# Window attention: band mask by a TensorE matmul, exponentials 1024 wide, maxima's rows from GpSimd's queue, longer lags

## What is computed

```python
scores = jnp.einsum('bhqd,bhkd->bhqk', q, k) / math.sqrt(dh)
scores = jnp.exp(scores - jnp.max(scores, axis=-1, keepdims=True))
d = j - i
mask = (d <= half - 1) & (d >= -half)
scores = jnp.where(mask, scores, 0.0)
weights = jax.nn.softmax(scores, axis=-1)
out = jnp.einsum('bhqk,bhkd->bhqd', weights, v)
...
return out.transpose(0, 2, 1, 3).reshape(B, S, H * dh) @ Wo
```

## Time and profile before

| what | value |
|---|---|
| median of 3 executions | 2661.12 us (2660.02 to 2675.28) |
| profiled execution, its own time | 2644.6 us |
| its span | 2642.8 us |
| mean granted TensorE clock | 0.842 |
| TensorE matmuls / weight loads busy | 2100.6 / 1602.7 us |
| VectorE busy | 1811.0 us |
| ScalarE busy | 1392.7 us |
| GpSimd busy | 659.4 us |

### The profile page before, as it was taken

The page is one execution under the profiler, slowest core; times in us unless marked ns, Lnnn a source line. Parts: engine busy times, 40 slices in busy tenths (PEclk is TensorE's granted clock), DMA queues, the critical chain, the costliest instruction groups (busy, mean ns, idle before and its releaser), DMA issues. The chain is left out here.

```text
span 2642.8 us, 46194 instructions
## 1 busy us (share of the span) xinstructions
PE 2100.6 (79%) x13533; PEld 1602.7 (61%) x13533; DVE 1811.0 (69%) x4451; ACT 1392.7 (53%) x2671; POOL 659.4 (25%) x920
## 2 busy tenths in 40 slices
PE   4779888788788898887888668356468848999998
PEld 2345556455555555564555657346467748999997
DVE  3667788778787787787968335536558745777775
ACT  3557667757666676676756212124246533444442
POOL 3110111101111111111100035555521135556511
PEclk8878888989888888898978555667679879999999
DMA  4624643565346435543470081699977742333311
GB/s 72 94 47 67 111 56 62 88 94 70 64 73 111 54 59 94 83 63 70 68 111 18 17 259 70 212 380 341 287 253 248 231 151 84 88 98 100 97 53 39
DMA packets 230094, 306.36 MB, mean 116 GB/s; under 512 B 44445, under 2 KB 145866, under 8 KB 229450
## 3 DMA queue, kind: packets, MB, share of 16 engines
q1 hardware_dynamic: 186746, 199.14, 37.5%
q0 software_dynamic: 22784, 67.13, 7.9%
q10 hardware_dynamic: 20304, 36.97, 3.7%
HBM read 129.33 MB, written 92.27 MB: 84 GB/s over the span
## 5 line engine op out<-in xcount | busy, mean ns | idle before, releaser
L724 DVE CUSTOM_DVE_ANT_0 above<-p_half,above 128x512 f32<-128x512 f32 x1024 | 691.3, 684 | 305.6 <-issue 248.1
L615 ACT ACTIVATE above<-p_diff 128x512 f32<-128x512 f32 x1024 | 599.4, 600 | 269.4 <-PE p_diff L529 267.6
L529 PE MATMUL p_diff<-d_stack,q_stack 96*128 96x512 bf16 x1024 | 433.3, 426 | 127.0 <-ACT above L615 96.0
L533 PE MATMUL p_half<-k_stack,q_stack 96*128 96x512 bf16 x1024 | 431.8, 422 | 31.0 <-DVE row_max L724 27.2
L558 PEld LDWEIGHTS p_pv<-v_win,w_win 128*128 128x128 f32 x2048 | 312.0, 225 | 78.0 <-DVE w_win L758 52.6
L558 PE MATMUL p_pv<-v_win,w_win 128*128 128x34 f32 x2048 | 307.6, 302 | 14.5 <-DVE w_win L758 13.0
L529 PEld LDWEIGHTS p_diff<-d_stack,q_stack 96*128 96x128 bf16 x1024 | 127.0, 125 | 285.3 <-ACT above L615 206.4
L1170 POOL DMA_INDIRECT raw<-sorted_y,place x192 | 206.2, 1074 | 238.5 <-DMA sorted_y<-y_tile 182.9
L641 ACT ACTIVATE p_win<-p_win 128x512 f32<-128x512 f32 x256 | 150.3, 589 | 181.5 <-PE p_win L545 179.9
L421 POOL TENSOR_TENSOR att<-total,inv 128x128 f32<-128x128 f32 x128 | 48.9, 404 | 759.2 <-DVE inv L750 759.2
L1492 ACT ACTIVATE pt_hi<-p_one 128x512 fp32r<-128x512 f32 x128 | 69.6, 595 | 259.6 <-PE p_one L1352 243.9
(11 more groups left out here) (217 smaller groups left out, 4857.1 us busy)
## 6 DMA issues: line engine op xcount, KB each, us to landing
x_tile<-sorted_x SPq DMA_DIRECT2D x141, 256.0 KB
sorted_y<-y_tile ACTq DMA_DIRECT2D x141, 256.0 KB
q_stack<-q_parts SPq DMA_DIRECT2D x256, 96.0 KB, 3.1
k_stack<-k_parts SPq DMA_DIRECT2D x256, 96.0 KB, 3.7
x_in<-in_L_attn_x SPq DMA_DIRECT2D x16, 1024.0 KB, 5.5
x_rows<-x POOLq DMA_DIRECT2D x16, 1024.0 KB
sorted_x<-zeros SPq DMA_DIRECT2D x51, 256.0 KB
d_stack<-d_parts SPq DMA_DIRECT2D x256, 48.0 KB, 3.7
```

The source lines that it names most:

```text
L529: nc.tensor.matmul(p_diff[s % 2][:], qs, d_stack[0:SPLIT_ROWS, h, :], start=True, stop=True).then_inc(s_diff, 1)
L533: nc.tensor.matmul(p_half[s % 2][:], qs, k_stack[g][0:SPLIT_ROWS, h, HALO + S // 2:HALO + S], start=True, stop=True).then_inc(s_half, 1)
L615: nc.scalar.activation(above[:, s % 4], p_diff[s % 2][:], ACT.Relu).then_inc(s_above, 1)
L724: nc.vector.tensor_tensor_reduce(out=above[:, s % 4], in0=p_half[s % 2][:], in1=above[:, s % 4], scale=1.0, scalar=-3.0e38, op0=ALU.add, o ...
```

## The change

The band becomes a bf16 tile `outside`, 0 in the band and -30000 outside. TensorE opens each bank of p_win with a matmul of the identity (bf16) and this tile, 512 columns, and the eight window matmuls of the bank add to it. The first exponential then gives 0 outside the band and the second 1, so VectorE only adds -1, in place in SBUF. Both exponentials are one instruction of 1024 columns, the second writes w_win. The second copies of the parts move from VectorE to GpSimd. The three row DMAs move from SyncE's queue to GpSimd's, behind the low part that they store. The lags change: exponentials 10 and 12, weights 14, weighted values 16 and 17, total 20, reciprocal and products 21.

```diff
-WIN_LAG, TOTAL_LAG, PAIR_LAG = 9, 18, 19
-EXP_LAGS = 10, 11, 12, 13
-WEIGHT_LAGS = 13, 14
-PV_LAGS = 15, 16
+WIN_LAG, TOTAL_LAG, PAIR_LAG = 9, 20, 21
+EXP_LAGS = 10, 12
+WEIGHT_LAG = 14
+PV_LAGS = 16, 17
...
-                if not isinstance(b, int) or 1 <= u <= 2 * B:
-
-                    wait_alone(sp, s_mparts, u)
-                    for part in range(3):
-                        row = SPLIT_ROWS + part
-                        sp.dma_start(q_stack[1 - g][row:row + 1, :, :],
-                                     m_parts[:, part, :]).then_inc(s_mrow, 16)
...
+                            pool.wait_ge(s_mparts, u)
+                            wait(pool, s_win, GH * (u - 2))
+                            alone(pool)
+                            for part in range(3):
+                                row = SPLIT_ROWS + part
+                                pool.dma_start(q_stack[1 - g][row:row + 1, :, :],
+                                               m_parts[:, part, :]).then_inc(s_mrow, 16)
...
+                            copy, of = (0, 1) if kind == "q" else (3, 2)
+                            nc.gpsimd.tensor_copy(parts[:, copy, cols], parts[:, of, cols]).then_inc(s_twice, 1)
...
-                wait(pe, s_ww, 2 * k)
+                wait(pe, s_e2, k)
                 for i in range(NBLK):
                     cols = slice(WIN * i, WIN * i + WIN)
+                    if i % 8 == 0:
+                        bank = p_win[:, 64 * i:64 * i + 512].rearrange("p (i j) -> p i j", j=WIN)
+                        nc.tensor.matmul(bank, ident_b[:], outside[:].unsqueeze(1).to_broadcast([P, 8, WIN]),
+                                         start=True, stop=False, skip_group_check=True)
                     ins = nc.tensor.matmul(p_win[:, cols], k_stack[o][0:ROWS, h, WIN * i:WIN * i + P],
-                                           q_stack[o][0:ROWS, h, cols], start=True, stop=True)
+                                           q_stack[o][0:ROWS, h, cols], start=False, stop=i % 8 == 7,
+                                           skip_group_check=True)
...
                 if again:
-                    act.wait_ge(s_e1, 2 * k + bank + 1)
-                    nc.scalar.activation(p_win[:, cols], p_win[:, cols], ACT.Exp).then_inc(s_e2, 1)
+                    act.wait_ge(s_e1, k + 1)
+                    wait(act, s_pv, k - 1)
+                    nc.scalar.activation(w_win[:, h % 2], p_win[:], ACT.Exp).then_inc(s_e2, 1)
...
-                nc.vector.scalar_tensor_tensor(
-                    w_win[:, h % 2, cols].rearrange("p (i j) -> p i j", j=WIN),
-                    p_win[:, cols].rearrange("p (i j) -> p i j", j=WIN), 1.0,
-                    window[:].unsqueeze(1).to_broadcast([P, NBLK // 2, WIN]),
-                    ALU.subtract, ALU.mult).then_inc(s_ww, 1)
+                dve.wait_ge(s_e2, k + 1)
+                nc.vector.tensor_scalar(w_win[:, h % 2], w_win[:, h % 2], -1.0, None, ALU.add).then_inc(s_ww, 1)
```

More of the change, by code:

```diff
@@ L36 @@
 PROJ = "qkd"
[L39 to L42 removed]
+OUTSIDE = -30000.0
+WIN_LAG, TOTAL_LAG, PAIR_LAG = 9, 20, 21
+EXP_LAGS = 10, 12
+WEIGHT_LAG = 14
+PV_LAGS = 16, 17
 STACK_INC = 16 * 6
@@ L113, in window_attention @@
         ones = sb("ones", [P, 1])
-        window = sb("window", [P, WIN])
+        ident_b = sb("ident_b", [P, P], BF16)
+        outside = sb("outside", [P, WIN], BF16)
         neg_half = sb("neg_half", [P, QT])
@@ L347, in _ @@
             const(nc.gpsimd.memset(ident[:], 0.0))
-            const(nc.gpsimd.memset(window[:], 1.0))
+            const(nc.gpsimd.memset(outside[:], 0.0))
             pool.wait_ge(s_const, 2)
@@ L351, in _ @@
                                           base=0, pattern=[[-1, P]], channel_multiplier=1))
-            const(nc.gpsimd.affine_select(out=window[:], in_=window[:], compare_op=ALU.is_ge, fill=0.0,
+            const(nc.gpsimd.affine_select(out=outside[:], in_=outside[:], compare_op=ALU.is_ge, fill=OUTSIDE,
                                           base=0, pattern=[[-1, WIN]], channel_multiplier=1))
             pool.wait_ge(s_const, 4)
-            const(nc.gpsimd.affine_select(out=window[:], in_=window[:], compare_op=ALU.is_ge, fill=0.0,
+            const(nc.gpsimd.affine_select(out=outside[:], in_=outside[:], compare_op=ALU.is_ge, fill=OUTSIDE,
                                           base=WIN - 1, pattern=[[1, WIN]], channel_multiplier=-1))
@@ L500, in unit @@
                 if g == 1 and has(b, -1, 0):
+                    pe.wait_ge(s_const, 17)
                     pe.wait_ge(s_wlo, 4)
@@ L550, in weighted_values @@
                 k = GH * w + h
-                pe.wait_ge(s_ww, 2 * k + part + 1)
+                if part == 0:
+                    pe.wait_ge(s_ww, k + 1)
                 if h == 0:
@@ L628, in unit, with exponential @@
                                                  ACT.Copy).then_inc(s_mid, 1)
[L629 removed]
+                    for n in (0, 1):
                         for w, o, h in late(b, g, s, EXP_LAGS[n]):
[L631 to L635 removed]
+                            exponential(GH * w + h, h, n)
+            def exponential(k, h, again):
                 if again:
[L637 to L638 removed]
+                    act.wait_ge(s_e1, k + 1)
+                    wait(act, s_pv, k - 1)
+                    nc.scalar.activation(w_win[:, h % 2], p_win[:], ACT.Exp).then_inc(s_e2, 1)
                 else:
                     act.wait_ge(s_win, k + 1)
[L641 removed]
+                    nc.scalar.activation(p_win[:], p_win[:], ACT.Exp, scale=DH ** -0.5).then_inc(s_e1, 1)
             batches(act, unit)
@@ L731, in unit @@
                             job(b, g, j, kind, i)
-                    for j, kind, i in jobs(b, g, s, 4):
-                        if kind in PROJ:
-                            dve.wait_ge(s_mid, before(PROJ, b, g, j) + 1)
-                            parts = {"q": q_parts, "k": k_parts, "d": d_parts}[kind]
-                            copy, of = (0, 1) if kind == "q" else (3, 2)
-                            cols = slice(512 * i, 512 * i + 512)
-                            nc.vector.tensor_copy(parts[:, copy, cols], parts[:, of, cols]).then_inc(s_twice, 1)
-                    for n in (0, 1):
-                        for w, o, hh in late(b, g, s, WEIGHT_LAGS[n]):
-                            weights(GH * w + hh, hh, n)
+                    for w, o, hh in late(b, g, s, WEIGHT_LAG):
+                        weights(GH * w + hh, hh)
                     for w, o, hh in late(b, g, s, TOTAL_LAG):
@@ L751, in unit, with weights @@
                                                  total[:, hh // 2 % 2, :, DH]).then_inc(s_inv, 1)
-            def weights(k, h, bank):
-                cols = slice(512 * bank, 512 * bank + 512)
-                dve.wait_ge(s_e2, 2 * k + bank + 1)
-                wait(dve, s_pv, k - 1)
-                nc.vector.scalar_tensor_tensor(
-                    w_win[:, h % 2, cols].rearrange("p (i j) -> p i j", j=WIN),
-                    p_win[:, cols].rearrange("p (i j) -> p i j", j=WIN), 1.0,
-                    window[:].unsqueeze(1).to_broadcast([P, NBLK // 2, WIN]),
-                    ALU.subtract, ALU.mult).then_inc(s_ww, 1)
+            def weights(k, h):
+                dve.wait_ge(s_e2, k + 1)
+                nc.vector.tensor_scalar(w_win[:, h % 2], w_win[:, h % 2], -1.0, None, ALU.add).then_inc(s_ww, 1)
             def totals(b, w, o, h):
```

13 lines of the change are left out of this document (5 added, 8 removed).

## The result

The change makes the kernel slower: 2746.57 us, the median of 4 executions, against 2663.91 us for the kernel before on the same chip, a ratio of 1.0314 (95% interval 1.0264 to 1.0364), or +82.7 us. The forecast was 2643 us in a range of 2560 to 2712. The profiled execution of the changed kernel took 2746.77 us.

A forecast was written before the change was run, and what follows sets the result against it. No engine was taken as full: heads were TensorE's burst plus VectorE's tail, with VectorE bounding heads with copies. Terms -61.5 - 50 + 102 + 13 - 21 = -17.5 us took the median 2661.1 to 2643 us, range 2560 to 2712.

The forecast's parts named there:

- Rows and copies: Row DMAs and second copies moved to GpSimd: VectorE's rows wait mostly goes, -61.5 us; copies leave VectorE, -50 us.
- Weights: One 1024-wide VectorE weight per head from SBUF takes 0.69 us, saving 65 us of VectorE, but nothing in the forecast sum.
- Mask, lags and burst: TensorE's mask matmuls and later lags leave VectorE fewer maxima inside the burst: 0.8 us a head, +102 us.
- Job T0: At lag 21 TensorE waits for GpSimd's products at T0: 1.6 us in each of 8 units, +13 us.
- Clock: Without the copies, a third of the 64 us held in low-clock stretches comes back: -21 us.
- slower by the burst: Rival: each head costs the full 1.1 us (141 us) and no clock comes back: 2703 us, chance 0.17.

The follow-up runs named there:

- b_both: Kernel before with only the maxima's row DMAs issued by GpSimd's queue and the second copies made by GpSimd; ratio 0.9775 to the kernel before.
- a_tot: Changed kernel with totals and head pairs' products back at lags 18 and 19; ratio 1.0171 to the kernel before.
- b_rows: Kernel before with only the maxima's three row DMAs moved to GpSimd's queue; ratio 0.9857 to the kernel before.
- a_short: Changed kernel with all lags of before (weight 13, weighted values 15 and 16, totals 18, pairs 19); ratio 1.0077 to the kernel before.
- s_halves: a_short with exponentials and weights cut into halves of 512 again, mask still on TensorE; ratio 0.979 to the kernel before.
- s_wwhalf: a_short with the weights alone in halves of 512, exponentials still 1024 wide; ratio 0.994 to the kernel before.
- a_fill: Changed kernel with ten unread matmuls on TensorE just before its wait for GpSimd's product at group 0's job T0; ratio 1.0202 to the kernel before.
- a_nomask: Changed kernel without its two mask matmuls per head, so the band isn't masked; ratio 1.010 to the kernel before.
- s_nomask: a_short without its two mask matmuls per head, so the band isn't masked; ratio 0.9927 to the kernel before.
- a_early: Changed kernel with the mask matmuls issued at lags 5 and 6 in place of 9; ratio 0.9942 to the kernel before.
- h_early: s_halves with the mask matmuls issued at lags 5 and 6, before the window scores; ratio 0.9582 to the kernel before.

## Why the prediction was wrong

By its own steps, with 1% as 26.6 us. The sum that the runs show is -60 (b_both) + 105 (a_tot less b_both, 3.96%) + 38 (the changed kernel less a_tot, 1.43%) = +83, in place of -17.5. The first layers of the traces give -51, +88 and +43. The intervals of the ratios leave each of the last two terms open by some 20 us. Of the 100 us between forecast and result, 51 lie in the saving of rows and copies, 25 in the lag of totals and products, 21 in the clock.

- **Rows and copies, "-61.5" and "-50"**: failed, -60 together. Rows are worth 38: a wait of 2 us is left where I took 1.5, as the window starts 3.1 to 4.4 us after the last issue and not 1.84, though the issues themselves are quicker than feared (0.62 us in the mean, not the 0.94 of the earlier trace rows). And VectorE lacks work for longer than TensorE waits, since the burst behind runs at half clock: in b_rows the eight longest of the gaps that summed to 73.5 us still sum to 33.7, where I left 12. "Nearly all comes back" was wrong for the copies: in a head bound by VectorE 0.64 of some 1.7 us come back before TensorE's chain bounds, and nothing in the head of job d shown for b_both. The term took the busy time of the removed instructions; it should have been the shorter of that and the distance to the next bound.
- **Weights, "0.69" and "I cost it at nothing"**: the size was right, 0.69 us alone, and "nothing" was wrong. With the lags of before the weighted values wait 0.22 us for the whole tile in the quiet head, where nothing stands beside it, and in one piece it costs 1.4%. Beside GpSimd's work it took up to 1.51 us in a_short and up to 1.01 in the changed kernel.
- **Mask, lags and burst, "+102"**: the size held, 105 measured (88 in the traces), and so did the quiet head, 9.09 + 1.1 = 10.19. Its parts did not. I had no term for ScalarE: "exponentials are no longer than the pairs that they replace ... nothing" was a wrong step. Their sum is no longer, but one piece of 1.06 us lets no Relu in between, and with the lags of before that is 1.5%. The lag of weights and weighted values, on which most of my chain rested (0.61 us a head), is 0.9%, or 0.19 us a head. The quiet head at full clock shows it part by part: 9.09 us in b_both, 9.34 in s_halves, 9.58 in s_wwhalf, 9.85 in a_short, 9.69 in a_tot, 10.19 in the changed kernel. The lag of weights and weighted values takes 0.16 us off it; the lag of totals and products adds 0.5, the largest part. That the total came out is luck in good part.
- **Job T0, "+13"**: failed, 38 for the lag of totals and products. I took a wait of 1.6 us, it is 2.7, and I priced the wait without the half clock that follows it. a_fill removes 1.1% of the 1.4% and leaves the products as late as they were. With the clock kept, T0's head is 1.52 us longer than with the old lag (11.16 against 9.64), 12 us in 8 units: the wait by itself was sized about right, the clock was the missing term.
- **Clock, "-21"**: failed. The clock fell, to 0.85 in the stretch where it was 0.86, and none of the 14 heads of job d came to full clock. Without copies it does not rise there: b_both has the same 0.64. The masks do go with a higher clock, 0.85 against 0.83 in a_nomask and 0.88 against 0.84 in s_nomask, but the waits at T0 bring it down again: a_tot has 0.87. The same masks moved out of the burst gave 0.91 in a_early and 0.93 in h_early.

The rival "slower by the burst" had the side, and heads of 10.19 us at full clock. Its mechanism, the step that the later weights take from VectorE, is the 0.9%. Its 2703 us still lay 44 below, since it too counted rows and copies in full and T0 as a bare wait.

What stays open: the prices of single parts depend on what they stand beside, so they are those along this one path of edits. Whether the first exponential or the second costs the 1.5% wasn't tried, nor why the later totals lengthen the quiet head by 0.5 us.

## What to carry to other kernels

Price an added instruction by where it stands: the two masks cost nothing in a wait of TensorE and 0.44 us a head in its burst, and with the masks there, the tiles in halves and the old lags, a change that lost 3.1% gains 4.2%. On an engine that serves a short recurring request, such as the Relu here, two short instructions can be better than one long one of the same sum; with the lags of before they were, by 1.5%. And a removed instruction is worth only the way to the next bound, for which a window of the busy times of all engines gives a first estimate before the edit.

## What the runs showed of the hardware

- A wait of TensorE of 2 us was followed by 1.2 GHz for the burst behind it: p_half 0.63 us for 0.38, weighted values 1.90 for 1.06. With matmuls in place of the wait at T0, the clock stayed at 1.00. Work that nobody reads made the kernel 1.1% faster.
- VectorE's subtraction on f32 in SBUF and GpSimd's copy lengthened each other. In a_short the weight at 522.92 took 1.51 us beside GpSimd's subtraction and copy, against 0.69 alone, and the copy 1.07, against 0.61 alone. GpSimd's subtraction stayed at 1.16 us. The weights of b_both, which read PSUM, took 0.67 to 0.69 us with GpSimd's work beside them or without. The weight and the copy in a_short:

```profile
522.72 1.16 POOL L402 TENSOR_TENSOR q_parts<-rest,q_parts 128x512 bf16<-128x512 f32 x1 [0.27 <-ACT q_parts L640]
522.92 1.51 DVE L760 TENSOR_SCALAR w_win<-w_win 128x1024 f32<-128x1024 f32 x1
523.82 1.07 POOL L405 COPY q_parts<-q_parts 128x512 bf16<-128x512 bf16 x1
```

- PSUM kept a mask that was written 3 to 4 steps before the scores were added to it, with matmuls into other banks between, in h_early and a_early.
